# Four-tile routing and an earlier second mixing in the middle stage of a Flamingo-like kernel

## The reference, cut to what matters

```python
x = x + tanh(g_xattn[0]) * attention(layernorm(x), ctx, ctx)             # stage 1
x = x + tanh(g_ffn[0]) * experts0(layernorm(x), ...)                     # 8 experts, top 2
x = x + tanh(g_xattn[1]) * layernorm(layernorm(x) + summary) * gamma...  # per batch, one summary row
x = x + tanh(g_ffn[1]) * experts1(layernorm(x), ...)                     # 64 experts, top 4, capacity 128

# experts1: flat is [2048, 512]
logits = flat @ Wr + router_bias
topk_scores, topk_idx = top_k(softmax(logits), 4)        # scores are normed over the 4
pos = running count of tokens per expert - 1             # over all tokens in order
valid = pos < 128
xb[eid, pos] = flat[tok]; yb = (silu(xb @ Wg) * (xb @ Wu)) @ Wd
out[tok] += yb[eid, pos] * w * valid
out += (silu(flat @ Sg) * (flat @ Su)) @ Sd              # 2 shared experts, hidden size 512 each
```

## Time and profile before

| what | value |
|---|---|
| median of three runs | 1297.86 us |
| profiled execution, own time | 1295.5 us |
| its span, first to last instruction | 1293.7 us |
| PE busy | 1094.5 us (85%) |
| DVE busy | 744.5 us (58%) |
| POOL busy | 571.2 us (44%) |
| ACT busy | 485.8 us (38%) |
| mean granted clock of PE | 0.945 |

### The profile page before, as it was taken

One profiled execution on the slowest core, in us unless ns is written; L12 is line 12 of the kernel. 1 busy time (PEld: TensorE's weight loads), 2 busy tenths in 40 slices (PEclk: granted clock), 3 DMA queues, 4 the chain that ended last, 5 costly groups with the idle time before them and its releaser, 6 DMA issues. The chain is left out here.

```text
span 1293.7 us, 19914 instructions
## 1 busy us (share of the span) xinstructions
PE 1094.5 (85%) x5479; PEld 752.2 (58%) x5479; DVE 744.5 (58%) x1760; ACT 485.8 (38%) x865; POOL 571.2 (44%) x754
## 2 busy tenths in 40 slices
PE   3998999999749999997896699998088788888984
PEld 2555555555247777773594376774076566666852
DVE  4678788786337888884665286675222222222556
ACT  2555556555227888884321212112022122221000
POOL 6455556554335667675136456563400000000775
PEclk9999999999969999998798799999599999999988
DMA  8554434441543333324221120211399999995776
GB/s 313 191 163 163 137 110 142 164 162 66 179 146 123 106 105 105 105 97 145 97 74 57 38 95 24 82 61 35 123 320 326 308 321 311 329 329 194 219 226 205
DMA packets 112117, 210.26 MB, mean 163 GB/s; under 512 B 15549, under 2 KB 23741, under 8 KB 112058
## 3 DMA queue, kind: packets, MB, share of 16 engines
q1 hardware_dynamic: 96058, 166.43, 38.4%
q0 software_dynamic: 16000, 43.13, 10.5%
HBM read 141.23 MB, written 77.59 MB: 169 GB/s over the span
## 5 line engine op out<-in xcount | busy, mean ns | idle before, releaser
L1975 POOL DMA_INDIRECT y<-ytab,take x64 | 69.4, 1084 | 285.1 <-POOLq L1814 265.9
L953 POOL TENSOR_TENSOR m_down_lo<-wo,m_down_hi 128x512 fp32r<-128x512 f32 x80 | 133.0, 1683 | 80.9 <-ACT m_down_hi L1028 80.9
L2040 PE MATMUL bank<-flat_hi,w_hi 128*128 128x512 f32 (+1 forms) x320 | 116.1, 363 | 12.8 <-DVE sh_h_b L2051 6.3
L471 PE MATMUL bank<-win,vT 128*128 128x512 f32 x256 | 124.1, 597 | 0.0
L1931 DVE TENSOR_TENSOR stage_gate<-stage_gate,bank 128x128 f32<-128x128 f32 x64 | 18.4, 287 | 176.0 <-ACT stage_gate L1908 176.0
L2040 PE MATMUL bank<-flat_hi,w_lo 128*128 128x512 f32 (+1 forms) x320 | 113.2, 354 | 0.0
L2040 PE MATMUL bank<-flat_lo,w_hi 128*128 128x512 f32 (+1 forms) x320 | 113.2, 354 | 0.0
L641 DVE TENSOR_REDUCE negmax<-bank 128x1 bf16<-128x512 f32 x128 | 86.9, 679 | 38.9 <-PE bank L478 38.5
L564 ACT ACTIVATE win<-bank 128x512 f32<-128x512 f32 x128 | 69.4, 594 | 97.2 <-PE bank L463 96.7
L1042 DVE TENSOR_TENSOR m_up_lo<-w,m_up_hi 128x1024 fp32r<-128x1024 f32 x80 | 99.0, 1239 | 10.3 <-ACT m_up_hi L1015 8.4
L1875 PEld LDWEIGHTS bank<-ident,m_x 128*128 128x128 f32 x256 | 36.7, 209 | 108.7 <-DMA m_x<-tab 96.9
(11 more groups left out here) (286 smaller groups left out, 2594.5 us busy)
## 6 DMA issues: line engine op xcount, KB each, us to landing
m_x<-tab SPq DMA_DIRECT2D x104, 256.0 KB, 3.5
tab<-zeros SPq DMA_DIRECT2D x16, 1024.0 KB, 10.3
ytab<-summary SPq DMA_DIRECT2D x64, 256.0 KB, 5.4
ytab<-m_y SPq DMA_DIRECT2D x40, 256.0 KB, 2.0
wout<-in_ctx SPq DMA_DIRECT2D x64, 128.0 KB, 2.6
w<-in_L_ffn_wi SPq DMA_DIRECT2D x16, 512.0 KB, 5.2
wo<-in_L_ffn_wo SPq DMA_DIRECT2D x8, 512.0 KB, 7.0
wout<-in_ctx SPq DMA_DIRECT2D x16, 256.0 KB, 3.2
```

The costliest lines, as they stand in the source:

```text
L471: nc.tensor.matmul(pO[s * 2 + h][:], vT[:, s, sb_, h:h + 2, :].rearrange("p a c -> p (a c)"), probs[:, sb_ % 2, h, :], start=(sb_ == 0), s ...
L953: nc.gpsimd.tensor_tensor(dn_lo[:, m, :], row(wo0, e * MB + m), dn_hi[:, m, :], ALU.subtract).then_inc(dn_lo_ready, 1)
L1975: nc.gpsimd.indirect_dma_start(y1[:, t % RING, k, :], None, T["ytab1"], bass.IndirectOffsetOnAxis(take1[:, t, k:k + 1], 0)).then_inc(gathe ...
L2040: last = nc.tensor.matmul(out, w[:, k, s, wc], x[:, d, cols], start=(d == 0 and part == 0), stop=(d == DB - 1 and part == 2))
```

## The change

- Routing handles the four tiles of a group at once. `choose` is cut in two (`choose`, up to the indices, and `mark`, one-hot rows and mask), `place` in `find` and `place`. One DVE instruction over 1024 elements per partition replaces 16 small ones for the one-hot rows and for the reading of places. The mask and slots are signalled once per group. PE's `positions` does 14 matmuls in one go: behind chunk 2 of the second half in group 0, behind chunk 0 elsewhere. All four logits of group 0 stand behind chunk 7 of its first half.
- The combines of group 1 move under the first half of group 0, its norms and summary under the second half, so that `flattened(0)` stands directly behind the last product and before the adds. `attended` is no longer part of `flattened`.
- On POOL, gathers wait tile by tile. Those of group 1 go between the powers of tiles 2 and 3 of group 0. The scatters of group 0 are issued in one go of 16 behind the sums of group 1; those of later groups stay in halves, but both halves come behind one slot signal.
- `inverse_std` loses its epsilon addition and its drain; the addition is now on DVE, in `statistics`, behind a drain.
- Weight splits 0 and 1 stand between the statistics of tiles 0 and 1, after a wait for the first gathers.
- In `up`, the product with `Su` comes before that with `Sg`, and the parts (high x high, high x rest, rest x high) are the outer loop.
- In groups 1 and 2, all mixing steps come one chunk later, and ACT's first normed tiles behind gate 4 instead of gate 3 (group 1's behind gate 0 of the second half instead of gate 7).

The diff, cut to its core (of `choose`, `place` and POOL's program only the new text is shown, and names of enlarged buffers are left out):

```diff
-        PLACED = {0: 0, 1: 1, 3: 2, 4: 3}
         groups_done = B - 1
-        NORMED = ((3, 7), (7, 7))
+        NORMED = ((4, 7), (0, 7))
...
         def logits_of(j):
-            return (pL, pC)[j // 2][:, j % 2 * E1:j % 2 * E1 + E1]
+            return pL[:, j * E1:j * E1 + E1]
+        def places_of(j):
+            return pC[:, j * E1:j * E1 + E1]
...
             def inverse_std(k, a=0, z_=TPB):
                 pool.wait_ge(var_ready, k + 1)
-                nc.gpsimd.tensor_scalar(ve[:, a:z_], mv[:, a:z_, 1], LN_EPS, None, ALU.add)
-                pool.drain()
                 nc.gpsimd.tensor_tensor(rstd[:, a:z_], ve[:, a:z_], power[:, a:z_], ALU.pow).then_inc(rstd_ready, 1)
             pool.wait_ge(T["s_zero1"], 16 * (ZERO_CHUNKS + 1))
...
+            def gather(n, tiles):
+                for j in tiles:
                     if n == 1:
+                        pool.wait_ge(x2_full, j + 1)
                     elif n > 1:
+                        pool.wait_ge(x2_ready, TPB * (n - 2) + j + 1)
+                    for k in range(2):
...
+            def dispatch(g, tiles):
+                pool.wait_ge(slot_ready, g + 1)
+                for j in tiles:
+                    for k in range(TOP1):
...
+            def sum_up(n):
+                inverse_std(stat(n - 1, 0))
+                for j in range(TPB):
+                    if n == 1 and j == 0:
+                        pool.wait_ge(summary_ready, B)
+                    pool.wait_ge(z_ready, (n - 1) * TPB + j + 1)
+                    nc.gpsimd.tensor_tensor(z[:, j, :], z[:, j, :], summary[:, n, :], ALU.add).then_inc(y_ready, 1)
+                for j in range(TPB):
+                    nc.gpsimd.tensor_tensor(x_sb[:, n * TPB + j, :], x_sb[:, n * TPB + j, :], beta[:],
+                                            ALU.add).then_inc(xb_ready, 1)
+                inverse_std(stat(n - 1, 1))
+            def keep_low(n):
+                inverse_std(stat(n - 1, 2))
+                for j in range(TPB):
+                    pool.wait_ge(fT_ready, TPB * n + j + 1)
...
+            gather(0, range(TPB))
+            for k in range(3):
+                inverse_std(first_stat(0, k), 0, 2)
+            gather(1, (0, 1))
+            inverse_std(first_stat(2, 0), 2, 4)
+            gather(1, (2,))
+            inverse_std(first_stat(2, 1), 2, 4)
+            gather(1, (3,))
+            inverse_std(first_stat(2, 2), 2, 4)
+            pool.wait_ge(beta_ready, 1)
+            sum_up(1)
+            dispatch(0, range(TPB))
+            keep_low(1)
+            for n in range(2, B):
+                gather(n, range(TPB))
+                dispatch(n - 1, (0, 1))
+                sum_up(n)
+                dispatch(n - 1, (2, 3))
+                keep_low(n)
+            dispatch(B - 1, range(TPB))
             pool.wait_ge(scattered, 16 * TILES * TOP1)
...
-            def positions(g, j):
-                need(pe, mask_ready, g * TPB + (j + 1))
-                if j:
-                    need(pe, pos_read, g * TPB + j)
-                nc.tensor.matmul(pL[:, 0:E1], before[:], mask[:, j, :], start=True, stop=False)
-                nc.tensor.matmul(pL[:, 0:E1], onesb[:], chosen[:, j % 2, :], start=False, stop=True).then_inc(pos_full, 1)
+            def positions(g):
+                need(pe, mask_ready, g + 1)
+                need(pe, pos_read, g)
+                for j in range(TPB):
+                    nc.tensor.matmul(places_of(j), before[:], mask[:, j, :], start=True, stop=False)
+                    for i in range(j):
+                        nc.tensor.matmul(places_of(j), onesb[:], mask[:, i, :], start=False, stop=False)
+                    last = nc.tensor.matmul(places_of(j), onesb[:], chosen[:], start=False, stop=True)
+                last.then_inc(pos_full, 1)
...
-            within = {(0, 0): ((with_beta, 2), (with_beta, 3)), (0, 1): ((logit, 0), (logit, 1)),
-                      (0, 5): ((transposed, 2), (transposed, 3)), (0, 7): ((logit, 2), (logit, 3))}
-            placed_first = {2: 0, 3: 1, 5: 2, 6: 3}
+            within = {(0, 0): ((with_beta, 2), (with_beta, 3)), (0, 5): ((transposed, 2), (transposed, 3)),
+                      (0, 7): [(logit, j) for j in range(TPB)]}
...
-                            if g == 0 and half == 0 and n in (0, HSH // P):
-                                pe.wait_ge(lo_ready, NSH + 1 + n // (HSH // P))
                             gate, up = gate_up(g, n)
-                            shared.up(pe, chunk(g, n, half), n, gate, up, cols, fresh=(half == 0 and n < 2))
+                            split = (lo_ready, NSH + 1 + n // (HSH // P)) if g == 0 and half == 0 and n in (0, 4) else None
+                            shared.up(pe, chunk(g, n, half), n, gate, up, cols, fresh=(half == 0 and n < 2), split=split)
...
-                            if half == 1 and n in placed_first:
-                                positions(g, placed_first[n])
-                        elif routed(g) and n in PLACED:
-                            positions(g, PLACED[n])
+                            if half == 1 and n == 2:
+                                positions(g)
+                        elif routed(g) and n == 0:
+                            positions(g)
...
                                 flat_tile(0, j)
+                        if g == 0 and half == 0 and n == 5:
                             for j in range(2, TPB):
...
-            split(0)
...
-            split(1)
...
+            def choose(g):
+                need(dve, lg_full, g * TPB + TPB)
+                nc.vector.tensor_tensor(logits[:], pL[:, 0:TPB * E1].rearrange("p (j e) -> p j e", j=TPB),
+                                        bias_r[:].unsqueeze(1).broadcast_to([P, TPB, E1]), ALU.add)
+                dve.drain()
+                for j in range(TPB):
+                    nc.vector.max(m8[:, j, :], logits[:, j, :])
+                dve.drain()
+                for j in range(TPB):
+                    nc.vector.max_index(i8[:, j, :], m8[:, j, :], logits[:, j, :])
+                nc.vector.tensor_copy(top1[:, g * TPB:g * TPB + TPB, :], m8[:, :, 0:TOP1])
+                dve.drain()
+            def mark(g):
+                nc.vector.tensor_copy(idxf[:], i8[:, :, 0:TOP1])
+                dve.drain()
+                shape = [P, TPB * TOP1, E1]
+                nc.vector.tensor_tensor(onehot[:].rearrange("p j k e -> p (j k) e"), iota_e[:].unsqueeze(1).broadcast_to(shape),
+                                        idxf[:].rearrange("p j k -> p (j k)").unsqueeze(2).broadcast_to(shape), ALU.is_equal)
+                dve.drain()
+                nc.vector.tensor_tensor(pair[:], onehot[:, :, 0:2, :], onehot[:, :, 2:4, :], ALU.add)
+                dve.drain()
+                nc.vector.tensor_tensor(mask[:], pair[:, :, 0, :], pair[:, :, 1, :], ALU.add).then_inc(mask_ready, 1)
+            def find(g):
+                need(dve, pos_full, g + 1)
+                nc.vector.tensor_tensor(junk[:].rearrange("p (j k) e -> p j k e", j=TPB), onehot[:],
+                                        pC[:, 0:TPB * E1].rearrange("p (j e) -> p j e", j=TPB).unsqueeze(2).broadcast_to(
+                                            [P, TPB, TOP1, E1]), ALU.mult).then_inc(pos_read, 1)
+                dve.drain()
+                nc.vector.tensor_reduce(posf[:], junk[:], AX.X, ALU.add)
+                dve.drain()
+            def place(g):
+                at = slice(g * TPB, g * TPB + TPB)
...
+                dve.drain()
+                nc.vector.tensor_tensor(slot1[:], by_tile(slotf), by_tile(drop), ALU.add).then_inc(slot_ready, 1)
+                nc.vector.tensor_scalar(posf[:], posf[:], float(CAP1 - 1), None, ALU.min)
+                dve.drain()
+                nc.vector.scalar_tensor_tensor(take1[:, at, :], idxf[:], float(CAP1), by_tile(posf), ALU.mult, ALU.add)
+                for j in range(TPB):
+                    nc.vector.tensor_tensor(chosen[:], chosen[:], mask[:, j, :], ALU.add)
                     dve.drain()
...
             def statistics(k, tiles=tuple(range(TPB))):
                 dve.drain()
                 for j in tiles:
-                    last = nc.vector.bn_aggr(mv[:, j, :], bn[:, j, :])
-                last.then_inc(var_ready, 1)
+                    nc.vector.bn_aggr(mv[:, j, :], bn[:, j, :])
+                dve.drain()
+                a, z_ = tiles[0], tiles[-1] + 1
+                nc.vector.tensor_scalar(ve[:, a:z_], mv[:, a:z_, 1], LN_EPS, None, ALU.add).then_inc(var_ready, 1)
                 dve.wait_ge(rstd_ready, k + 1)
...
             def mix_in(a):
                 tiles = (a, a + 1)
+                if a == 0:
+                    dve.wait_ge(gathered[0], 16 * 2)
                 for j in tiles:
+                    if a == 0:
+                        split(j)
                     dve.wait_ge(x2_full, j + 1)
                     nc.vector.bn_stats(bn[:, j, :], x2_bank[j][:])
                 statistics(first_stat(a, 0), tiles)
...
```

(76 more changed lines are left out.)

109 lines of the change are left out of this document (22 added, 87 removed).

## The result

The changed kernel takes 1287.28 us (median of 20 runs, 1284.26 to 1300.84) where the kernel before takes 1295.26 (20 runs beside it). The ratio is 0.9947, 95% interval 0.9927 to 0.9968, so the change saves 6.9 us, between 4.1 and 9.5 (the medians lie 8.0 apart). All comparisons of traces are therefore made from the start of the middle stage, POOL's MEMSET of `power` (595.02 before, 601.05 after). A second profile of the same changed kernel (experiment 1, span 1284.7 us) is the control.

A forecast was written before the change was run, and what follows sets the result against it. PE was the engine to follow, with long waits of 21.3 and 23.9 us. Terms -4.0 - 0.3 - 2.7 + 2.4 = -4.6 on the profiled 1295.5 gave 1290.9; with the median 2.4 higher, forecast 1293.2 us, range 1284 to 1301.

The forecast's parts named there:

- rival B: Gaps before powers stay near 1.5 us since the bulk load ends early: -10.0, 1287.9 us; chance 0.25.
- a price of the first power after gathers or scatters: POOL's gap before such powers, 1.47 to 3.89 us, blamed on the preceding DMA_INDIRECT, not the drain, and kept.
- rival A: POOL's drain causes the gaps, which go with it: entry -3.3, stalls 1.7, total -16.7, 1281.2 us; chance 0.08.
- First half of group 0: PE waits 8.4 us for sums and products 1 and 2 behind gapped powers; slow clock adds 1.0.
- T0: End of the last logits of group 0, closing its first half: 664.4 before, predicted 673.3.
- Second half, T0 to transposes: 16 scatters before power 2 come late next; 7 us of PE's 21.3 us wait stay, transposes at T0 + 45.8.
- Entry: 595 to 633 us: gathers end 2.8 us earlier without two splits, epsilon moves save 0.15 each; taken as -0.5.
- Clock: Down matmuls after PE's long wait: a hole of 7 us keeps most of the 2.8 us slow-clock loss, -0.3.
- Rival C: Starts and stops hold PE at half clock through group 0's first half: +1.9, 1299.8 us; chance 0.17.
- Groups 1 and 2: PE's waits among the chunks vanish with compact routing and later mixing: -1.5 and -1.2, together -2.7 us.
- rival E: Mask and flat tiles come late in groups 1 and 2, +3 for -2.7: +1.1, 1299.0 us; chance 0.10.
- the tail: Last logits to first scatter: routing becomes serial behind the last logits, 10.2 us instead of 7.8, +2.4.

The follow-up runs named there:

- experiment 1: The changed kernel run again with no edit, as control with a second trace: 1288.87 us, ratio 0.9958 to the kernel before.
- Experiment 3: The kernel before with only the epsilon addition moved to DVE and POOL's drains at the powers removed: 1291.55 us, ratio 0.9984.
- experiment 2: The changed kernel with POOL's drain put back in front of each power, epsilon staying on DVE: 1292.84 us, ratio 0.9995 to the kernel before.
- experiment 5: The changed kernel with one POOL drain where POOL idles, before the wait for group 3's slots: 1279.33 us, ratio 0.9881 to the kernel before.
- experiment 6: The changed kernel with one POOL drain ahead of the gathers of group 3, so 40 transfers follow it: 1290.92 us in one run.
- experiment 9: The kernel before with the epsilon on DVE, no drains at the powers, and one POOL drain where it waits for the last slots: 1284.66 us, ratio 0.9922.
- experiment 4: The changed kernel with group 1's norms, sum and attention back behind group 0's last product, group 0's scatters in halves: 1291.25 us, ratio 0.9977 to the kernel before.
- experiment 7: The changed kernel with four of group 0's 16 scatters (tile 0) issued early, before the second power of the sum: 1281.25 us, ratio 0.9897 to the kernel before.
- experiment 10: The changed kernel with weight splits 0 and 1 back at the start of DVE's queue: 1287.21 us, ratio 0.9936 to the kernel before.
- experiment 11: The changed kernel with group 0's positions behind chunk 3 instead of 2, find and place behind product 3: 1283.31 us, ratio 0.9899 to the kernel before.
- experiment 8: The changed kernel with an idle-place POOL drain, tile 0's scatters early and group 0's positions behind chunk 3: 1272.84 us, ratio 0.9831 to the kernel before.

## Why the prediction was right, and where its steps failed

The time was right (1293.2 forecast, 1287.3 measured, within 1284 to 1301), and the sign. But this was in good part luck. The sum came near through errors of both signs, up to 13 us in one term. The forecast also started from 1297.86 for the kernel before, which took 1295.26 beside the changed one; 2.6 of the 5.9 us between forecast and measurement are that. And the measured time lies nearest to rival B's 1287.9, whose gaps near 1.5 us did not occur.

**The step that failed: "I read it as a price of the first power after gathers or scatters".** It was the drain. Experiment 3 takes only the drain and its addition away and all gaps go; experiment 2 puts the drain back, without the addition, and they return. The row that had spoken for my reading, 0.15 behind the same drain where no DMA_INDIRECT came before, fits as well: there had been no transfer since the drain before it. I had weighed "drain" against "DMA before it" as two rivals, when it is the product of both. Thus rival A, which I gave 0.08, named the cause: its entry of -3.3 lies between what the two traces show at chunk 0 (-2.2 and -5.3), its stalls of 1.7 are 0.4 and 0.5.

**First half of group 0, +8.9 predicted.** Without gaps PE lost 0.36, and T0 came 1.1 earlier, 4.2 in the control. The gathers put ahead of the powers cost nothing: DVE's input came later than they ended (POOL idles 0.77, 3.54 and 2.98 before the three powers behind them in the changed kernel). This term was 10 to 13 us off.

**A term that stood nowhere: +6.5 at the end of the stage.** Nothing in the sum asked what else the removed drains had done. Each had paid for the transfers since the drain before it; without them the price of 96 falls due in one go, between the last scatter and the first expert load, where nothing hides it. Experiments 5, 6 and 9 show it. It is also the larger part of why A's 16.7 did not come; the mask wait took 4.0 more.

**Second half, T0 to transposes: -12.9 predicted, -8.8 measured in both runs.** The mechanism held: the 16 scatters in front of power 2 are late next, and 6.0 of the long wait stay where 7 were predicted (experiments 4 and 7). The size was off by the mask wait, 4.36 against 0.4 predicted: product 4, put at T0 + 16.3, came at T0 + 21.4, and power 1 was done at T0 + 26.0 instead of T0 + 21. The missing gap of 1.8 before power 2 gave a part of that back. I had placed POOL's additions correctly, up to T0 + 14 (684.69 is T0 + 15.4), and routing beside them, but priced the routing as undisturbed. Onehot, pair and mask took 4.73 there and 1.94 in experiment 4, and the cast before them 0.84 instead of 0.17. In place's rows the same effect stood before me.

The Trainium skill, "SBUF — State Buffer", section "SBUF: two separate sides", says that a DVE operation with two SBUF inputs and a GpSimd operation that reads SBUF exclude each other for a whole instruction. The trace agrees: POOL's four additions at 673.52 took 5.04 and the four at 678.53, beside onehot, pair and mask, 6.16, while each of those three took 0.9 to 1.0 more than in experiment 4. I had used the rule for gathers beside splits and not for this, where it mattered more.

**Entry, -0.5 predicted.** The 2.8 us that the gathers were to end earlier did not come: their last one ends 15.1 us after the stage's start and 15.2 before. The prediction weighed the rule for the gathers of group 1 beside splits 2 and 3, but the gathers of group 0 meet splits 0 and 1 at their new place as well, and two are stretched as before (experiment 10). With the drain gone chunk 0 came 3.0 earlier in experiment 3 and 5.1 in experiment 9, which have no other part of the change; the two traces of the changed kernel have 2.2 and 5.3, so what is won fits the drain alone.

**Clock.** Rival C fell. The windows of the changed kernel (columns as in the earlier trace rows):

```profile
636.00:638.00 2.00, 0.88 (x4) 0.50 1.04 384
655.00:657.00 2.00, 2.00 (x19) 1.00 0.00 0
...
683.00:685.00 2.00, 2.00 (x12) 0.53 0.03 8
...
719.00:721.00 2.00, 1.78 (x9) 0.50 0.00 0
```

The clock was 0.50 for the first 5 us of the chunks, where the kernel before had it for 3, and full from there to T0. From chunk 0 to T0 it takes 32.2 us instead of 31.0 in both runs, and only 0.4 to 0.5 of that is the wait: C's mechanism cost at most 0.8 here, not the 4.6 at which it decides. After the mask wait of 4.36 the clock fell (0.53 over the two us from 683), which stood nowhere in the sum; after the 1.53 of experiment 11 it stayed at 1.00. After the wait of 6.0 it was at 0.50, and the 16 down matmuls took 8.58 where they took 7.03 at full speed and 8.94 stood in the earlier trace rows: a hole of 6 keeps 1.5 of the 1.9 lost, as predicted (-0.3).

**Groups 1 and 2, -2.7, and the tail, +2.4.** Measured: from the logits of group 1 to those of 2 it takes 76.83 instead of 78.59, from 2 to 3 76.82 instead of 78.21, -3.15 together; rival E fell. The tail is +1.8. Here DVE's timeline of the changed kernel bears the prices:

```profile
894.46 0.42 DVE L1550 TENSOR_TENSOR logits<-bank,bias_r 128x256 f32<-128x256 f32 x1 [0.98 <-PE bank L1370]
...
896.92 1.22 DVE L1566 TENSOR_TENSOR onehot<-iota_e,idxf 128x1024 bf16<-128x1024 f32 x1
...
901.37 1.22 DVE L1580 TENSOR_REDUCE posf<-junk 128x16 f32<-128x1024 f32 x1
...
903.07 0.18 DVE L1590 TENSOR_TENSOR slot<-slotf,drop 128x16 int32<-128x16 f32 x1
```

The 1024-wide operations take 1.22, as taken from the earlier trace rows. From the logits to the mask it was 4.55 (4.8 taken), and from there to the scatter 5.04 (5.4 taken).

**The parts, as far as the runs separate them.** Removing the drains alone saves 2 us (experiment 3, not separable from none); four-tile routing with the moved mixing and the drains kept saves 0.6 (experiment 2, the same); together 5 to 7. That they help each other, because the new order puts transfers ahead of the powers that PE waits for, is argued and not shown: the difference of some 3 to 4 us lies within what the intervals of the three ratios leave open. Four-tile routing was never run apart from the moved mixing; the tail, +1.8, is where it alone is seen. Within the changed kernel, moving the mixing early is worth 4.7 us up to the transposes and, by the medians of experiments 1 and 4, 2.4 in the time; with intervals of 2 us either way these do not contradict each other. The late positions of experiment 11 would have given 3.2 more. Not tried by themselves: the new order of the parts in `up`, the tile-wise gather waits, and the mixing steps one chunk later in groups 1 and 2.

## What to carry to other kernels

Where a wait appears only when two things meet, test the pair as one mechanism before choosing between them. Before a drain is removed from a queue that issues transfers, find the next place that drains and what stands behind it; if that is a stage's end, put one drain where the engine idles anyway. When work moves beside another engine's long run of operations, price it with the rows taken beside such a run.

## What the runs showed of the hardware

**The price of a drain on POOL.** A drain here costs about 0.082 us for each indirect transfer that POOL has issued since its last drain. The sign of it is the gap from the last scatter to the first expert load: 3.27, 5.23 and 9.79 us behind 16, 40 and 96 transfers in experiments 5, 6 and 1, kernels that differ only in the place of the last drain (the changed kernel's 96 count from the drain at the start of the stage). Over the ten other profiles it holds as well: 3.25 to 3.28 behind 16, 9.81 behind 96. It does not matter that most of the transfers have long landed: `flattened` waits until all scatters of the group before have landed, so 80 of the 96 were in place before the last group's scatters began.

**Where the drain stands.** No drain is written at the end of the stage. That one happens there is concluded from the price: the gap grows by the same 0.082 for each transfer, and a drain written earlier takes the growth away (experiments 5, 6, 8 and 9).

**In front of a power.** In experiment 2 the wait, counted from the input of the power or from the end of the last scatter, whichever is later, is 1.50 and 1.48 behind 16 transfers issued well before, where 16 x 0.082 gives 1.31 and 0.16 is what a power behind no transfer waits. Behind scatters that POOL issued just before, it is longer, 1.87 and 1.92 behind eight and 2.46 behind 16: about 1.0 more than the count gives. That this is the landing of the last of them was not tested.

**What stays open.** In the entry the count does not explain it: 2.86 behind eight, 4.85 behind four, 0.33 and 1.29 behind two. Loads into SBUF ran in a part of that stretch in the kernel before; that they are the reason was not tested. The 3.89 of the earlier trace rows, behind 16 transfers like the 1.47 a group earlier, is not explained either. Whether the price goes by transfers or by their rows (128 in each of them) stays open.
